# A ViT block on one core: values weighed in fp16 halves, relu's low half on VectorE, four stack buffers and a respaced attention order

## What is computed

```python
h = einsum('bhid,oi,od->bho', x, weighted_sum, weight)   # "mix"
qkv = layernorm(h) @ qkv_w.T + qkv_b                     # 16 heads of 16
q, k = rotate(q), rotate(k); q, k = q / |q|, k / |k|
attn = softmax(q @ k.T * 16 ** -0.5)
h = h + (attn @ v) @ out_w.T + out_b
x = layernorm(h)
w = where(sigmoid(x @ Wg + bg) > 0.5, sigmoid(x @ Wg + bg), 0)
h = h + sum_e w[:, e] * (relu(x @ W1[e] + b1[e]) @ W2[e] + b2[e])   # 8 experts, hidden 1024
```

## Time and profile before

| | |
|---|---|
| median of three runs | 1910.03 us |
| the profiled execution's own time | 1907.93 us |
| its span, first to last instruction | 1906.1 us |
| mean granted TensorE clock | 0.99 |
| PE busy | 1834.9 us, 96% |
| DVE busy | 697.6 us, 37% |
| ACT busy | 1077.5 us, 57% |
| POOL busy | 629.4 us, 33% |
| one expert's W1 or W2 from the issue of its load to landing (page, DMA issues) | 4.8 us, median |

### The profile page before, as it was taken

How to read it: one execution, slowest core, us unless ns; L and a number is a source line. 1 busy time by engine, 2 the same in 40 slices (tenths; PEclk the granted TensorE clock), 3 DMA queues, 4 the chain that set the end, 5 groups by cost and what they waited for, 6 DMA issues and landing times.

```text
span 1906.1 us, 31838 instructions
## 1 busy us (share of the span) xinstructions
PE 1834.9 (96%) x12652; PEld 1166.2 (61%) x12652; DVE 697.6 (37%) x1575; ACT 1077.5 (57%) x1658; POOL 629.4 (33%) x537
## 2 busy tenths in 40 slices
PE   5688999999999999999999999999999999999999
PEld 4156545775467754777457764577546775466666
DVE  7858645452123610336004450145402352121001
ACT  3744776546654576545664466544665546654444
POOL 1012323334233332333323342333423334234443
PEclk9789999999999999999999999999999999999999
DMA  4332542515123331334213251231512315113221
GB/s 164 113 109 89 147 164 89 188 67 133 67 89 100 100 100 67 111 100 106 95 67 111 100 133 47 107 113 56 133 67 89 122 68 133 67 67 110 101 102 43
DMA packets 103971, 192.31 MB, mean 101 GB/s; under 512 B 67448, under 2 KB 80656, under 8 KB 87440
## 3 DMA queue, kind: packets, MB, share of 16 engines
q1 hardware_dynamic: 103824, 190.28, 30.8%
HBM read 153.55 MB, written 20.97 MB: 92 GB/s over the span
## 4 chain that ended last, share of the span: by engine, by line
PE 83%; DVE 3%; ACT 3%; DMA 2%; issue 2%; SPq 0%; DVEq 0%; ACTq 0%
PE bank_h L994 31%; PE bank_f L1013 11%; PE bank_f L1015 10%; PE bank_f L1016 10%; PE bank_o L902 6%; PE bank_s L888 4%; PE bank_s L800 3%; PE bank_s L801 3%; PE bank_s L802 3%; DMA kt<-probs 1%; ACT hh L777 1%; DMA kt<-stack 1%; DVE acc L1254 1%; DMA raw<-in_w_dram 1%; PE bank_s L948 1%
## 5 line engine op out<-in xcount | busy, mean ns | idle before, releaser
L643 POOL TENSOR_TENSOR hl<-h,hh 128x512 f16<-128x512 f32 x512 | 602.7, 1177 | 1192.9 <-ACT hh L777 685.3
L994 PE MATMUL bank_h<-x,w1s 128*128 128x512 f16 x3072 | 749.0, 380 | 5.0 <-ACT hh L777 4.4
L774 ACT ACTIVATE h<-bank_h,b1s 128x512 f32<-128x512 f32 x512 | 351.3, 686 | 468.5 <-PE bank_h L994 468.3
L1013 PE MATMUL bank_f<-w2s,hh 128*128 128x256 f16 x2048 | 560.4, 274 | 0.8 <-DVE acc L1254 0.8
L1015 PE MATMUL bank_f<-w2s,hh 128*128 128x256 f16 x2048 | 558.7, 273 | 0.0
L1016 PE MATMUL bank_f<-w2s,hl 128*128 128x256 f16 x2048 | 558.7, 273 | 0.0
L994 PEld LDWEIGHTS bank_h<-x,w1s 128*128 128x128 f16 x3072 | 287.3, 98 | 330.2 <-issue 39.5
L777 ACT ACTIVATE hh<-bank_h,b1s 128x512 f16<-128x512 f32 x512 | 350.0, 684 | 0.0
L743 ACT ACTIVATE probs<-bank_s 128x1024 f32<-128x1024 f32 x240 | 246.4, 1026 | 167.3 <-PE bank_s L888 166.3
L1013 PEld LDWEIGHTS bank_f<-w2s,hh 128*128 128x128 f16 x2048 | 201.5, 98 | 105.0 <-issue 38.8
L1254 DVE SCALAR_TENSOR_TENSOR acc<-bank_f,gw,acc 128x256 f32<-128x256 f32 x256 | 106.2, 477 | 369.5 <-PE bank_f L1016 369.4
(11 more groups left out here) (187 smaller groups left out, 1436.5 us busy)
## 6 DMA issues: line engine op xcount, KB each, us to landing
w1s<-w_parts SPq DMA_DIRECT2D x56, 1024.0 KB, 4.8
w2s<-w_parts SPq DMA_DIRECT2D x56, 1024.0 KB, 4.8
raw<-in_w_dram SPq DMA_DIRECT2D x16, 1024.0 KB, 6.6
xraw<-in_x_t_dram SPq DMA_DIRECT2D x30, 512.0 KB, 4.8
w_parts<-w1s SPq DMA_DIRECT2D x8, 1024.0 KB, 8.6
w_parts<-w2s SPq DMA_DIRECT2D x8, 1024.0 KB, 10.5
out_dram<-acc SPq DMA_DIRECT2D x16, 256.0 KB, 6.1
w1s<-in_x_t_dram SPq DMA_DIRECT2D x2, 512.0 KB, 8.2
```

The source lines that it names most:

```text
L643: pool.tensor_tensor(hl[n % HBUFS][:], h32[n % 2][:], hh[n % HBUFS][:], ALU.subtract)\
L774: act.activation(h32[n % 2][:], bank_h[n % 2][:, :], ACT.Relu, bias=b1s[:, e, m:m + 1]).then_inc(h_hi.sem, 1)
L994: last = pe.matmul(bank_h[n % 2][:, :], w[:, wp, k, m * P:(m + 1) * P], x16s[fb % 2][:, xp, k, :], start=(k == 0 and wp + xp == 0), stop=( ...
L1013: pe.matmul(o, high, w[:, 0, m, :], start=(m == 0 and t % 2 == 0), stop=False, skip_group_check=True)
```

## The change

For the attention of batches 2 to 7, values are kept as two fp16 halves (`v16`), and the exponentials too (`halves`). `weigh` becomes three fp16 passes of four matmuls (high by high, low v by high p, high v by low p) where it was one fp32 pass. ScalarE writes each exponential into one of three buffers (`exps`: parts of `qk`, and `stack`), and a new step `halves` has VectorE make the high half (a copy) and the low half (a subtraction) of each of the 32. So that v fits fp16 it is scaled by a power of two that is folded into the weights once (`v_max`, `scale_values`), during batch 0's last chunk. `relu_low` moves L643's subtraction from GpSimd to VectorE for batches 1 to 7, one place later in the list (the low half of chunk n - 1 at step `f1` n). There are four stack buffers, so no stack waits for a transpose. The turning of the stacks is put ahead of the load of expert 3 on SyncE. `split_ahead` splits the first x tile of the next batch ahead of `gates_turn`. The due times of batches 2 to 7 are new, and some of the preparation steps in batch 0 move.

```diff
-                  (9.0 - sooner + 1.5 * t, "ln1_turn", t), (10.55 - sooner + 1.5 * t, "qkv", t),
...
+        steps += [(mix[t], "mix", t), (turn + gap * t, "ln1_turn", t),
+                  (turn + 0.05 + gap * (t + 1), "qkv", t), (turn + 0.1 + gap * (t + 1), "rotate", t),
...
+        if later:
+            steps.append((first + pace * (n + 0.8), "halves", n))
...
-MIX = [2.1, 3.5, 4.9, 6.3]
+LATER_MIX = [0.6, 2.1, 3.2, 4.3]
+LATER_TURN, LATER_GAP, LATER_NORM = 6.7, 1.5, 13.4
+LATER_UNIT = [15.1, 16.3, 17.5, 18.7]
+LATER_FIRST, LATER_PACE = 21.4, 0.78
...
                 for e in range(2, EXPERTS):
-                    load_expert(b, e)
                     if more and e == 3:
                         turn_stacks(b + 1, range(TT))
+                    load_expert(b, e)
...
-                if stage == "f1":
+                if stage == "f1" and fb == 0:
...
-                        if n >= 2 and ab:
-                            wait(act, stack_turned[a], ab, 16 * (n - 1))
...
+                        terms = exps[n % 3]
+                        if n < 3:
+                            wait(act, qk_unit, ab, TT)
+                        else:
+                            wait(act, halved, ab - 2, n - 2)
...
-                        last = pe.matmul(bank_o[32 * j:32 * j + 32, :],
-                                         v1[:, tile, h, :, :].rearrange("p s d -> p (s d)"),
-                                         probs[n % 2][:, j, :], start=(tile == 0), stop=(tile == TT - 1),
-                                         skip_group_check=True)
+                        passes = [(v_high, p_high), (v_low, p_high), (v_high, p_low)]
+                    for k, (v, p) in enumerate(passes):
+                        for j in range(4):
+                            last = pe.matmul(bank_o[32 * j:32 * j + 32, :],
+                                             v[:, 4 * g + j].rearrange("p s d -> p (s d)"), p[:, j, :],
+                                             start=(tile == 0 and k == 0),
+                                             stop=(tile == TT - 1 and k == len(passes) - 1), skip_group_check=True)
...
+            def relu_low(fb, n):
+
+                if fb == 1 and n == 0:
+                    wait(dve, h_lo, fb, 0)
+                wait(dve, h_hi, fb, 2 * (n + 1))
+                wait(dve, f2_done, fb, n - HBUFS + 1)
+                dve.tensor_tensor(hl[n % HBUFS][:], h32[n % 2][:], hh[n % HBUFS][:], ALU.subtract)\
+                   .then_inc(h_lo.sem, 1)
...
+                if stage == "f1" and fb and n:
+                    relu_low(fb, n - 1)
...
+                elif stage == "split_ahead":
+                    if ab + 1 < BATCHES:
+                        split_x(ab + 1, 0, range(2))
...
+                        half_v.link(dve, dve.tensor_tensor(values, at_v[:, 0:D], qkvb[:, 2 * D:QKV], ALU.add))
+                        values = values.rearrange("p (h d) -> p h d", d=HD)
+                        half_v.link(dve, dve.tensor_copy(v16[:, 0, n, :, 0, :], values))
+                        dve.tensor_tensor(v16[:, 1, n, :, 0, :], values, v16[:, 0, n, :, 0, :], ALU.subtract)\
+                           .then_inc(v_out.sem, 1)
...
+                elif stage == "halves":
+                    u, half = divmod(n, 2)
+                    high, low = (halves[u % 2][:, part, 2 * half:2 * half + 2, :] for part in range(2))
+                    wait(dve, weighed, ab, u - 1)
+                    wait(dve, exped, ab, n + 1)
+                    half_v.link(dve, dve.tensor_copy(high, exps[n % 3]))
+                    dve.tensor_tensor(low, exps[n % 3], high, ALU.subtract).then_inc(halved.sem, 1)
```

More of the change, by code:

```diff
@@ L62, in attention_order @@
     steps = []
-    mix, sooner, att_at = (FIRST_MIX, 1.5, FIRST_ATT) if first_ffn else (MIX, 0.0, range(TT))
+    later = not alone and not first_ffn
+    sooner, att_at = (1.5, FIRST_ATT) if first_ffn else (0.0, range(TT))
+    mix, unit = (FIRST_MIX, [u - 0.6 * sooner for u in UNIT]) if first_ffn else (LATER_MIX, LATER_UNIT)
+    turn, gap, norm = (LATER_TURN, LATER_GAP, LATER_NORM) if later else (9.0 - sooner, 1.5, 15.7 - sooner)
     for t in range(TT):
-        steps += [(mix[t - 1] - 0.05 if t else 0.3, "split", t), (mix[t], "mix", t),
-                  (9.0 - sooner + 1.5 * t, "ln1_turn", t), (10.55 - sooner + 1.5 * t, "qkv", t),
-                  (10.6 - sooner + 1.5 * t, "rotate", t),
-                  (UNIT[max(t - 1, 0)] + 0.1 * min(t, 1) - 0.6 * sooner, "unit", t),
-                  (UNIT[t] + 0.3 - 0.6 * sooner, "stack", t)]
-    steps += [(6.8, "ln1", 0), (15.7 - sooner, "qk_norm", 0), (24.0, "out_bias", 0)]
+        steps += [(mix[t], "mix", t), (turn + gap * t, "ln1_turn", t),
+                  (turn + 0.05 + gap * (t + 1), "qkv", t), (turn + 0.1 + gap * (t + 1), "rotate", t),
+                  (unit[max(t - 1, 0)] + 0.1 * min(t, 1), "unit", t), (unit[t] + 0.3, "stack", t)]
+    steps += [(mix[TT - 1] + 0.5, "ln1", 0), (norm, "qk_norm", 0), (20.0 if later else 24.0, "out_bias", 0)]
     if alone:
@@ L94, in attention_order @@
               (tail + 13.7, "bias2", 0)]
+    steps.append((tail + 12.0, "split_ahead", 0))
+    if not alone:
+        steps += [(mix[t - 1] - 0.05, "split", t) for t in range(1, TT)]
     steps.sort(key=lambda s: s[0])
@@ L140, in merge @@
         return order
-    between = {("scores", 0): [("maxima", 0), ("maxima", 1), ("reduce", 0), ("scales", 0),
+    between = {("scores", 0): [("v_max", 0), ("maxima", 0), ("maxima", 1), ("reduce", 0), ("scales", 0),
                                ("parts", 0), ("parts", 1), ("parts", 2), ("parts", 3)],
@@ L439, in stack_of @@
         def stack_of(b, t):
[L441 removed]
+            if t < 2:
+                return stacks[t]
+            return more_stacks[:, t - 2] if b == 0 else spare_stacks[t - 2]
         def stack_slots(b, t, a):
@@ L1256, in steps @@
                            .then_inc(acc_done.sem, 1)
+                elif stage == "v_scaled":
+                    scale_values()
                 elif stage == "maxima":
```

125 lines of the change are left out of this document (96 added, 29 removed).

## The result

The changed kernel takes 1920.0 us (median of five executions, 1917.88 to 1921.31), the kernel before 1910.03 beside it: a ratio of 1.0048, with a 95% interval of 1.0037 to 1.0060. The change makes the kernel half a per cent slower. The profiled execution took 1917.88, 10.0 us more than the one of before; the spans differ by 10.0 as well (1916.1 and 1906.1). The forecast was 1926, or 1924.1 on the basis of the profiled execution of before.

The account below looks back on a forecast made before the run. TensorE was taken to bound the kernel, busy 228.7 of 230 us a batch. Terms sum to +2.9 a batch, +17.4 for six, -1.2 once: 1907.9 becomes 1924.1, median 1926 (own range 1917 to 1935; overall 1889 to 1948).

Parts of the forecast that it names:

- clock: TensorE's clock falls to half speed for 3.4 us behind most waits of 4.5 us: +1.7 a batch (0 to 5.1).
- weigh: Three fp16 passes replace one fp32 pass, 0.21 us less a unit, 16 units: -3.4 us a batch (-0.6 to -3.8).
- boundaries: TensorE's changes between whole and part array, 88 a batch against 81 before: +0.8 us a batch.
- once only: Outside the six batches: batch 1 saves 2.4 us, batch 0 pays 1.2 us for new preparation work; -1.2 in all.
- rival 2: The wait ahead of the first scores comes but the clock holds: +1.2 us a batch, 1916 us; chance 0.16.
- The way to the first scores: From A, VectorE's start on the last tile's qkv, through norm, stacks and transposes; TensorE waits 4.5 us (3.2 to 5.7).
- the accumulation at 888.19: VectorE's accumulation between norm and units moves behind the third stack, bringing the first transpose forward: -1.8 us.
- rival 3: The clock stays low as long as behind the 4.15 us wait, 5.1 lost, not 1.7: 1946 us; chance 0.12.
- VectorE in the scores stage: From first to last scores, VectorE is busy 82 us of TensorE's 90, at 92%: covered, but barely.
- Rival 4: VectorE becomes the bound of the scores stage, 8 us above TensorE: +50 us, 1976; chance 0.09.
- SyncE's order: Expert 3's W1 load, now issued later, stays hidden; it would cost only if it took over twice its 4.8 us.
- Rival 1: The transposes land in time, so waits and clock cost no more: -2.5 us a batch, 1894 us; chance 0.30.

Follow-up runs that it names:

- experiment 5: On top of experiment 1, the fourth unit and third stack are planned behind the second expert's accumulation, not ahead of it: 1890.21 us.
- experiment 4: Changed kernel, with ScalarE's order swapped in one more place: scores exponentials ahead of a relu when a halves step stands between: 1915.21 us.
- experiment 2: Changed kernel, with relu's low half formed by GpSimd in every batch again, not by VectorE: 1927.42 us.
- experiment 7: Changed kernel, with a batch's first x tile split inside the batch again, not behind the gates of the batch before: 1952.97 us.
- experiment 3: Changed kernel, weighing in one fp16 pass instead of three, so the output lacks the two low-half passes: 1881.23 us.
- experiment 1: Changed kernel, with a batch's first scores planned at 22.8 instead of 21.4 and pace 0.742 instead of 0.78: 1889.23 us.
- experiment 9: Changed kernel, with SyncE issuing expert 3's loads ahead of the transposes of q and k again: 1968.57 us.
- experiment 6: On top of experiment 5, the first scores planned still later, at 23.4 with pace 0.7255: 1897.56 us.
- experiment 10: Experiment 5 with the first scores planned at 23.1 and pace 0.7337: 1898.62 us.
- experiment 11: On top of experiment 5, transposes in batches 2 to 7 no longer wait for the previous landing into the same tensor: 1882.98 us.
- experiment 12: Changed kernel, with transposes in batches 2 to 7 no longer waiting for the previous landing into the same tensor: 1903.74 us.
- after: The changed kernel itself, without any follow-up edit: 1920.0 us.
- experiment 8: Changed kernel's order, stacks and splits, but one fp32 weigh pass, two exponential buffers and no halves in batches 2 to 7: 1967.13 us.

## Why the prediction was right, and where it was off

The sign and the mechanism were right, and the total (1924.1 against 1917.9 for the profiled execution) lies 6.2 us off. By the account above, measured less forecast: clock -5.4, weigh -2.1, boundaries and other work +1.7, waits 0.0 (six times 3.8, both), once only -0.4. The sign did not need the clock: without its 4.8 us the changed kernel would still be 5 us slower (an estimate from this account). The median, 1920, lies between the forecast and rival 2, in which the clock holds (1916), since it fell at half of the waits.

- **The way to the first scores: right, with one wait unseen.** First transpose at A + 11.7 predicted, A + 11.6 measured; from there to the scores 15.0 predicted, 14.4 in this batch and 15.2 on the mean of the six (14.4 to 16.3); TensorE would have asked at A + 22.2 and would have been there at A + 22.4. But the waiting of 4.5 us falls apart into two: 1.53 ahead of an `f2`, then 2.8 at the scores, 4.4 together. The step "the accumulation at 888.19 now comes behind the third stack: -1.8" booked this move only as a gain for the chain. It did not ask who waits for the accumulation. In the sum it did no harm, because every microsecond waited there is one less at the scores; experiment 5 shows exactly that exchange. It did harm in another way: a chain bound by two waits keeps the second when the first is cured. And that the sum of the waits comes out to a tenth is luck in part, since the late landings decide it in three batches of six.
- **The clock: a term twice too large.** +1.7 a batch was forecast, 0.8 measured: it fell in three batches of six. "Most waits of 4.5 us should do this" had no row for a wait that is split in two. The waits at which it held are 2.06, 2.02 and 3.09, those at which it fell 2.29, 3.64 and 3.90, so the length of the wait at the scores does not sort them. In experiment 4 it fell at 3.65, 3.52 and 3.49 and held at 3.55. The Trainium skill, TensorE: Matmul & The Clock Gate, section "Part 1: The HAM clock gate", makes idling return the engine to the low clock; the trace agrees for three waits of six. This is 5.4 us of the 6.2. The argument against rival 3 also misread its window: of the 10.3 us at 0.50, the 1.3 in which TensorE did nothing are the end of the wait itself, and behind it TensorE was busy for 9.0 of 9.0. So that row does not show "thin work", and in experiments 2 and 7 the clock did stay low for 7 us in dense work, twice in each.
- **Weigh: 0.235 where 0.21 was taken**, 2.1 us in all. The fixed part is some 0.12, close to the boundary that the working had as its other bound (experiment 3).
- **The boundaries: a wrong count.** The working has 88 changes between whole and part array and 81 "now"; the lists, and the order of the matmuls in both traces, have 80 and 66. Fourteen more at 0.11 would have been +1.5 a batch in place of +0.8. Measured is +1.1 for all of TensorE's work other than weigh, so the small error in the sum is luck.
- **The exponential in chunk 22:** 0.53 measured, 0.5 forecast; experiment 4 removes it.
- **VectorE in the scores stage:** 82 of 90 us forecast, 78.5 of 90.6 measured, and it is not the bound: experiments 1 and 3. Rival 4 is refuted up to a stage squeezed to 85.9 us (experiment 1). A batch's 185 was too high by 15, of which the halves, at 1.86 us each in place of 1.95, are only 3; a low half costs VectorE 0.63, and its other work fell from 74.9 to 69.1 us a batch with GpSimd idle.
- **Once only:** -1.2 forecast, -1.6 measured. The chunks with batch 1's attention take 3.1 us less (2.4 forecast): the waits of 2.34 and 2.45 are gone, and a fall of the clock with them, while two waits of 1.3 and 1.4 for an accumulation and one of 1.8 for a relu are there. Batch 0's own attention takes 1.6 more, 1.1 of it ahead of the first matmul, which the working does not name.
- **SyncE's order: costed at nothing, and worth 49 us** if undone alone (experiment 9). The prediction asked only whether the load of expert 3 would come too late behind the transposes; it did not ask what the old order would cost in the new list. That the load behind them is not free either shows as soon as TensorE comes sooner (experiments 6 and 10).
- **"Four buffers don't shorten this: each transpose still waits for the one before."** Right, and it was the most valuable sentence of the working: experiments 11 and 12 take that wait away.
- **Rival 1** (1894) did not come about, but it described the kernel that experiment 1 makes, 1889: transposes that land in time. The profiled execution of experiment 1, 1889.8, is 2 us under what rival 1 gives on that basis, 1891.7.

## What to carry to other kernels

When a change shortens the time between two hand-overs of a critical engine, write down for each step of the chain between them the time at which it is ready and at which it is asked for, and list everyone who waits for an instruction that is moved back, not only what is moved forward. Here the 21.4 chunks of front were 1.4 too few, and that cost more than the 23 us that weigh gained. When one wait is cured, expect the next one behind it at once (accumulation, transposes, weights: experiments 1, 5, 6); only shortening the chain itself, here by an unneeded wait between transposes into different parts of a tensor, gained at both places where it was tried (experiments 11 and 12).

## What the runs showed of the hardware

- **A packet of the instruction queue goes with a late transpose.** In after's six batches the wait at the scores is 2.0 to 2.3 us where the DMA view shows no packet of the instruction queue q8 during the transposes, and 3.1 to 3.9 where it shows one. Two windows of the changed kernel, 661 to 667 and 1120 to 1127 us, in the second and in the fourth batch:

```profile
q1 hardware_dynamic: 3799, 0.94, 81.4%
```

```profile
q1 hardware_dynamic: 3412, 0.85, 86.8%
q8 instruction: 1, 0.02, 0.8%
```

The same holds in experiments 3 and 4: of 18 batches, the ten with such a packet wait 3.1 to 3.9 us, the eight without it 2.0 to 2.3. In experiment 12 it is 1.4 to 1.5 against 1.0. In the kernel before, all six batches have such a packet and a landing of 3.9 to 5.1 us, but TensorE comes later and waits 0.6 at most. There are exceptions: in the fourth batch of experiments 5, 6, 10 and 11 the packet is there and no landing is late, and in the last of experiment 8 TensorE waits 3.3 us behind a landing of 4.2 without one. So it is no more than a correlation; no run moved the packet by itself.
- **Which wait lowers the clock.** Waits of 1.53 never did, waits of 3.2 in dense work five times in six (experiment 2), and of those at the scores 3.09 and 3.55 did not, where 2.29 did (changed kernel, experiment 4). The shortest at which it fell was 2.09 (experiment 7); 2.75 ahead of the first mix did it six times in six (experiment 7). What else counts stays open.
- **A transpose that shares the DMA engines with a load of 1 MB** took twice as long: 6.5 us from the first to the second into `qt`, against 3.3 (experiment 9).
